# A hint for the branch back in the pass loops of a four-layer GNN kernel

## The reference

```python
h = relu(layernorm(x));  x = x + hgcn(h, W[0..2], b, edge_weight, src, dst)   # 3 rounds of: matmul, ball arithmetic,
                                                                              # agg = segment_sum(w * ht[dst]) at src
h = relu(layernorm(x));  x = x + attention1(h, edge_attr_16, ...)             # e = leaky(er[dst] + el[src, edge])
                                                                              # alpha = softmax of e over each dst
                                                                              # out = segment_sum(alpha * x_t[src]) at dst
h = relu(layernorm(x));  x = x + mlp(h, edge_attr_8, ...)                     # msg = relu([x[src], x[dst], ea] @ W1) @ W2
                                                                              # out = segment_sum(msg) at dst
h = relu(layernorm(x));  x = x + attention2(h, ...)
# hgcn, one round:
msgs = edge_weight[:, None] * ht[edge_col]
agg = segment_sum(msgs, edge_row, num_segments=6250)
# attention:
ex = exp(e - segment_max(e)[dst]);  alpha = ex / segment_sum(ex)[dst]
```

## The kernel before

| pass | VectorE | TensorE | ScalarE | GpSimd |
|---|---|---|---|---|
| 0 (gcn) | 259, then 222 | 552 | 5 | 59 |
| 1, 2 (gcn) | 238 | 554 | 5 | 59 |
| 3 (att) | 488 | 729 | 229 | 66 |
| 4 (mlp) | 294 | 650 | 81 | 67 |
| 5 (att) | 470 | 730 | 232 | 67 |

## Time and profile before

### The profile page before, as it was taken

One profiled execution on the slowest core, in us unless ns is written; L12 is line 12 of the kernel. 1 busy time (PEld: TensorE's weight loads), 2 busy tenths in 40 slices (PEclk: granted clock), 3 DMA queues, 4 the chain that ended last, 5 costly groups with the idle time before them and its releaser, 6 DMA issues.

```text
span 14736.1 us, 379076 instructions
## 1 busy us (share of the span) xinstructions
PE 9514.2 (65%) x89162; PEld 8562.9 (58%) x89163; DVE 10167.6 (69%) x46548; ACT 4152.8 (28%) x13780; POOL 10586.9 (72%) x10932
## 2 busy tenths in 40 slices
PE   0000007777778888788887888887555555888887
PEld 0000006777767777677776777776444444777777
DVE  7870007777776666766667787878766766888887
ACT  1000000000000000000002777776222222777777
POOL 3777777777767777677776777775777776777776
PEclk9985558888888888888886555555555555555555
DMA  2101112222111111111111111111111111111111
GB/s 100 26 25 26 26 28 46 41 42 41 37 27 27 27 27 27 27 27 27 27 27 27 27 26 26 26 26 20 31 28 27 28 28 28 28 27 27 27 27 27
DMA packets 500039, 447.85 MB, mean 30 GB/s; under 512 B 291533, under 2 KB 316749, under 8 KB 498254
## 3 DMA queue, kind: packets, MB, share of 16 engines
q0 software_dynamic: 349696, 337.89, 13.8%
q1 hardware_dynamic: 149454, 102.38, 2.5%
HBM read 368.39 MB, written 65.20 MB: 29 GB/s over the span
## 4 chain that ended last, share of the span: by engine, by line
PE 37%; issue 20%; DVE 18%; POOL 12%; DVEq 8%; DMA 3%; ACT 1%; POOLq 0%; ACTq 0%; SPq 0%
PE bank L1463 16%; PE bank L1438 12%; POOL packed L423 9%; DVEq L705 3%; DMA G<-table,idx 3%; POOL G L442 3%; PE bank L1520 3%; PE bank L1532 3%; DVE OH L722 2%; PE bank L1509 1%; DVE OHB L733 1%; PE bank L1451 1%; PE bank L1536 1%; DVEq L707 1%; DVE OHT L761 1%
## 5 line engine op out<-in xcount | busy, mean ns | idle before, releaser
L442 POOL DMA_INDIRECT G<-table,idx x9360 | 9063.1, 968 | 3426.3 <-issue 2429.8
L1463 PE MATMUL bank<-UZ,OHT 128*128 128x192 bf16 x15600 | 2095.3, 261 | 540.6 <-DVE OHT L761 540.6
L1438 PE MATMUL bank<-G,OH 128*128 128x64 f32 x9984 | 1674.1, 299 | 586.8 <-DVE OH L722 466.0
L423 POOL DMA_INDIRECT packed<-Y,slab_pos x1568 | 1523.6, 972 | 671.4 <-issue 495.3
L1356 ACT ACTIVATE OHB<-bank,const 128x512 bf16<-128x512 f32 x159 | 109.2, 687 | 6711.7 <-PE bank L1451 6711.7
L1463 PE MATMUL bank<-UZ,V 128*128 128x192 bf16 x14976 | 1999.0, 260 | 0.0
L1438 PEld LDWEIGHTS bank<-G,OH 128*128 128x128 f32 x9984 | 1486.9, 216 | 753.8 <-DVE OH L722 686.9
L1463 PEld LDWEIGHTS bank<-UZ,OHT 128*128 128x128 bf16 x15600 | 1511.6, 111 | 580.3 <-DVE OHT L761 558.0
L1438 PE MATMUL bank<-ZR,OH 128*128 128x65 f32 x6656 | 1765.4, 419 | 0.0
L1438 PEld LDWEIGHTS bank<-ZR,OH 128*128 128x128 f32 x6656 | 1623.6, 334 | 0.2
L722 DVE TENSOR_SCALAR OH<-const,DL,W 128x128 f32<-128x128 f32 x4992 | 1560.6, 368 | 0.2 <-issue 0.2
(11 more groups left out here) (281 smaller groups left out, 18624.1 us busy)
## 6 DMA issues: line engine op xcount, KB each, us to landing
G<-table,idx POOLq DMA_INDIRECT x9360, 2.5
packed<-Y SPq DMA_DIRECT2D x42, 640.0 KB, 17.6
UZ<-packed SPq DMA_DIRECT2D x104, 256.0 KB, 2.7
Y<-in_payload SPq DMA_DIRECT2D x98, 256.0 KB
packed<-Y,slab_pos POOLq DMA_INDIRECT x1568
table<-Y SPq DMA_DIRECT2D x6, 1690.0 KB, 5.5
idx<-SRC SPq DMA_DIRECT2D x624, 8.0 KB
X<-in_x SPq DMA_DIRECT2D x1, 1568.0 KB, 7.9
```

Source lines behind the costliest of these rows:

```text
L423: pool.indirect_dma_start(out=packed_rows, out_offset=bass.IndirectOffsetOnAxis(ap=slab_pos[:, h, c:c + 1], axis=0), in_=slab[:, h, c, :], ...
L442: pool.indirect_dma_start(out=G[:, 2 * q + c, :], out_offset=None, in_=table, in_offset=bass.IndirectOffsetOnAxis(ap=idx[:, h, j:j + 1], a ...
L1438: o = pe.matmul(ps_a[r % 2][:, 0:w], OH[:, q, c, :], parts[c], start=c == 0, stop=c == 1)
L1463: o = pe.matmul(ps_rows[c // 2][:, c % 2 * 3 * D:(c % 2 + 1) * 3 * D], tile_hot(tile)[:, c * P:(c + 1) * P], table_parts[:, tile, :, :].re ...
```

## The change

`steps` makes its loop through another call, which writes one more instruction, `BRANCH_PREFETCH_HINT`, at the top of the loop's body. It names the loop's closing compare-and-branch. All else stays: the loops of GpSimd and SyncE, VectorE's of pass 0 and ScalarE's of the gcn passes.

```diff
             for u in range(BODY):
                 body(u, 0)
-            with eng.Fori(1, ITER) as i:
+            with nc.Fori(1, ITER, engines=[eng.engine], hint_back_edge=True) as i:
                 body(None, i)
             for u in range(lag):
                 body(u, ITER)
```

## The result

The changed kernel takes 14557.26 us (median of 4 runs, 14554.0 to 14585.36), the kernel before beside it 14731.44 us (median of 4, 14725.0 to 14737.74). The ratio is 0.9887, with a 95% interval of 0.9873 to 0.99: 174 us less, where 178 were forecast, for 14556. The total was right; three of its four terms were well off, and their errors cancelled. The profiled execution of after happens to be the longest of its four (14585.36, the others 14554 to 14559), so its own times add up to 153 us less than before's, not to 174.

What follows compares the result with a forecast made beforehand. GpSimd's fetches bound the gcn and mlp passes, VectorE the attention passes 3 and 5. 135 + 73 = 208, less 10 for waiting and 20 for loop ends, is 178: median 14556 us, range 14518 to 14690.

Steps and rivals of the forecast that it cites:

- The mechanism: VectorE's long attention loops lose their first block at the branch back; the hint has it at hand, chance 0.77.
- pass 4: VectorE's hole goes there too, but GpSimd bounds the pass: zero gain, bound 0 to 3 us.
- rival C: VectorE, passes 3 and 5: hint steers every fetch, blocks between come on demand; slower, 15434 us; chance 0.04.
- A: The hint changes nothing, the target's block still comes on demand: about 14750 us; chance 0.09.
- B: The hint works in pass 5 alone; in pass 3 the hole moves behind the first block: 14681 us; chance 0.08.
- Pass 3: VectorE sets the pace; its hole at the branch shrinks, saving 135 us, or 123 with GpSimd's slower fetches.
- with the block at hand there remain 0.45 us: VectorE's hole at the branch in pass 3, 3.22 us, shrinks to 0.45 us, saving 138 us.
- the hint itself: The hint instruction on VectorE in pass 3 costs some 0.06 us a turn, 3 us in all, at most 10.
- Pass 5: VectorE's hole goes, worth 123 us alone, but GpSimd becomes the bound: 73 us saved, lower bound 57.
- Mutual waiting: In pass 3 two engines at 40.4 and 40.6 us an iteration make each other wait at times: 10 us off.
- Loop ends: The block behind 14 hinted loops may be missing when the branch isn't taken: 0 to 39 us, taken +20.
- The other passes: VectorE's passes 1 and 2, all of TensorE and ScalarE: the hint's own cost is hidden, zero.

Runs made afterwards that it cites:

- p3_only: The kernel before with the hint in VectorE's loop of pass 3 alone: 14616.40 us, ratio 0.9923.
- p5_only: The kernel before with the hint in VectorE's loop of pass 5 alone: 14635.69 us, ratio 0.9930.
- rest_only: The changed kernel without the hint in VectorE's passes 3 and 5, twelve hints staying: 14752.56 us, ratio 1.0009.
- late3: The kernel before with one hint, VectorE's in pass 3, written ahead of the last of the 16 steps: 14728.13 us, ratio 0.9987.
- slot_hint: The changed kernel with VectorE's loop of pass 3 moved to the head of a 128-instruction fetch block: 14531.31 us, ratio 0.9863.
- slot_plain: The kernel before, no hints, with VectorE's loops of passes 3 and 4 moved to the head of a block: 14747.88 us, ratio 1.0006.
- step3x: The changed kernel with ten small VectorE copies more in pass 3, one in each of steps 2 to 11: 19899.93 us, ratio 0.9877, slow chip.
- step5x: The changed kernel with ten small VectorE copies more in pass 5, one in each of steps 2 to 11: 19947.83 us, ratio 0.9895, slow chip.
- pe_act: The kernel before with only the nine hints on TensorE and ScalarE: 20161.53 us, ratio 1.0004, slow chip.

## Why the prediction was right, and where not

*The mechanism* was right in each step: the target is fetched in place of the block behind the branch, at the entry of the branch's block; both attention passes gain; pass 4 gains nothing; rival C's fetches ahead go on. `p3_only`, `p5_only`, `rest_only` and `late3` show it. Rivals A, B and C are out.

*Pass 3, 135 us forecast; 101 in the two profiles, 116 in that of `p3_only`.* The failing term is "with the block at hand there remain 0.45 us", at 40.6 us an iteration. Measured 0.77 us before `DLw` (39.2 / 51): +0.32, of which 0.06 is the hint itself, for which the forecast had a term of its own; +0.26 remain. I had read what a branch costs in pass 1, whose loop needs no packet, but in pass 3 the block behind the target must still be fetched, at once after the branch. And I had left the rest of the body as it was, though the hints shift the blocks, so that a third entry costs its full price: +0.42 in the step table (34.04 to 34.46). 40.63 + 0.68 = 41.31 is the iteration measured. My 40.6 is reached where both are gone: 40.5 in `slot_hint`. `p3_only`, without the shift, lies between, at 41.03.

*Pass 5, 73 us forecast; 80 in the two profiles, 98 in `p5_only`.* The turn to GpSimd came as foreseen, and so did the end of VectorE's lag. Mis-sized was GpSimd's fetch, taken at 960 ns in the mean or, as a bound, at 970: it came down to 948 in `p5_only`. So the range of this term (57 to 73) looked to one side only. (The hole was 151.7 / 50 = 3.03 us and not 2.98, as one of the 51 waits lies outside the loop; with GpSimd as the bound this changes nothing.)

*Mutual waiting, 10 us.* There was no such cost to see. In pass 3 the two paces were 0.8 us apart (41.3 us an iteration for VectorE, 40.5 for GpSimd without its 22 us of waits) and not 0.2, so the term had nothing to act on; and `slot_hint`, where they meet, shows no such cost at 40.5 us either.

*Loop ends, 20 us.* The joints between passes grew by about 5 us in after, and by as much in `rest_only`. The 20 were too many. What the other hints did cost, about 13 us of `rest_only`'s 19, lies in passes 1 and 2, in GpSimd's fetches, where I had taken zero.

The errors, in the two profiles: pass 3 gave 34 us too little; pass 5 gave 7 more, the waiting cost 10 less and the ends 15 less, so these terms come to -176 where -178 was forecast. The other passes and the start, which I had at zero, cost 23 us in the profiles. Some 17 us of that, and 5 us of pass 5, are the slower fetches of that one execution, which the median doesn't have. That the median lies 1 us from the forecast is thus luck: 34 us too little in pass 3, against pass 5, the waiting and the ends, which add up to nearly as much the other way.

## What to carry to other kernels

A branch back that is followed by "issue" for some 3 us while instruction packets come in tells of a loop that doesn't stay in its engine's memory: count the packets of an iteration, and see at which instruction they come. The hint is worth its 0.04 us where that engine sets the pace, and nothing elsewhere; with the loop's head at the start of a block it is worth more, and a loop that then fits into three blocks needs no hint. Before the gain of such an edit is counted, take the bound of the pass from a row of the next slowest engine, and leave a per cent or two of that engine's own operation open in both directions. And before a small loss in several passes is put down to the edit, compare the median of one operation with other traces: here most of the loss was the execution's.

## What the hardware showed

- VectorE's instructions come in blocks of 8192 bytes, 128 instructions. A loop in three blocks stays whole (pass 4 in `slot_plain`), one in four takes 5 packets an iteration without the hint and none with it (pass 3 in `slot_plain` and `slot_hint`, with the hint even 499 instructions, pass 3 in `step3x`), one in five takes 6 without and 5 with it (pass 3 in before and after).
- A hint acts at the entry of the block that holds its branch. Written behind that entry it does nothing (`late3`), and a branch some 4 instructions behind the entry keeps 2.2 us of its hole (`step5x`).
- A block's entry costs VectorE 0.06 to 0.39 us when the block is fetched ahead, by where in a step of pass 3 it falls, and 0.10 to 0.13 us in `slot_hint`, where it is there.
- GpSimd's fetch of one and the same size took 948 to 965 ns in the mean in pass 5 and 964 to 977 in pass 4, in ten traces from ordinary chips; its ordinary 0.305 us in between didn't move. In a pass of 1664 fetches 10 ns are 17 us. One execution had 3 ns more in the median in five passes, 24 us in all. What moves the fetch is not shown.
- The same kernel took 14731 to 14747 us on three chips and 20151 us on a fourth. The traces there show GpSimd, VectorE and TensorE waiting for each other, while the single operations take about as long (in `pe_act` GpSimd's fetch 990 ns in the mean, 968 before; VectorE's write of `ZR` 283 ns, 285 before); the cause is open.
